# Order of the first loads and weights, and x added image by image, in a preactivation convolution on one core

## The chip, the cores and the metric

The kernel runs on one core of a Trainium2 chip. The metric is the device time of one execution in microseconds (us). Engines: TensorE (PE, matmuls; PEld, its weight loads), VectorE (DVE), ScalarE (ACT), GpSimd (POOL) and SyncE (SP, here only a queue that issues DMAs). ACT and POOL issue DMAs as well.

## The reference

x is 8 images of 32 channels, 64 x 64, float32. Each channel of each image is normalised over its pixels (a group norm with 32 groups of one channel), the image is split into its four parities (2 x 2 pixels become 4 x 32 = 128 channels of 32 x 32), and three depthwise convolutions (1x1, 3x3, 5x5) are joined to 384 features, projected by a 1x1 convolution to 128 channels, put back to 64 x 64, and added to x.

```python
g = (v - mean(v)) / sqrt(var(v) + 1e-5)                    # per image and channel
xd = concat([g[:, :, 0::2, 0::2], g[:, :, 0::2, 1::2], g[:, :, 1::2, 0::2], g[:, :, 1::2, 1::2]], axis=1)
feats = concat([dwconv(xd, w1, 1), dwconv(xd, w3, 3), dwconv(xd, w5, 5)], axis=1)
y = einsum('bchw,oc->bohw', feats, w_proj[:, :, 0, 0])
out[:, :, 0::2, 0::2], out[:, :, 0::2, 1::2], out[:, :, 1::2, 0::2], out[:, :, 1::2, 1::2] = split(y, 4, axis=1)
return x + out
```

## The kernel before

**Work.** The depthwise taps and the projection are folded where that pays. For the nine inner taps (distance at most 1) effective weights `weff` (projection scaled by w5, plus w3, for the centre also w1) are made on the chip and split into a high part `whi` and a low part `wlo`; the normalised image G is split into HI and LO in the same way, and PE accumulates HI x whi, HI x wlo and LO x whi: 3 x 9 taps x 2 banks of 512 columns = 54 matmuls an image (lines 657 to 706). The 16 outer taps of the 5x5 (the ring) are summed elementwise: ACT makes a scaled product for each of POOL's taps (line 430), POOL adds them into RING_SUM (line 316), DVE adds its own taps into ACC (lines 584, 592, 596), then F = ACC + RING_SUM (line 602), and PE projects F with one matmul a bank (`ring`, line 708). `POOL_N` says how many of the 16 taps of each image are POOL's, the first of them made by ACT straight into RING_SUM.

**Data.** X holds all images on the chip, two images to a pair t = b // 2 (64 partitions each, even rows on the first 32 of them, odd rows on the others). ACT copies the finished YP of image b into Y (`copy_y`, line 406; Y has room for two pairs), POOL starts a DMA that adds Y to X for a pair (`add_x`, line 322, places in `ADD_X_AT`: after sum (4, 2), (6, 2) and (7, 6)), and SP stores both images of the pair when it has landed (lines 246 to 249). Image 6 is added by POOL itself in two halves (lines 344 to 349), image 7 by DVE from PSUM (lines 620 to 626); each half is stored when it is done, by SP and, for half of image 7, by ACT. SP's stores are issued in the order of the program: pairs 0, 1, 2, then image 6, then image 7.

**Start.** Image 0's and image 1's statistics come from a second copy of the images, the parts XS (four parts of each channel on 128 partitions), by `part_bn`, a mask (`spread`) and a PE matmul (`sum_parts`, line 643); POOL takes the root by pow (`inv_std`), and DVE makes the bias (`part_bias`, line 500). SP issues w5, w3, the parts of image 0 in two pieces, the parts of image 1, images 1 to 7. ACT issues the projection, w1 and image 0. PE transposes the projection, then the coefficients (line 726), then sums the parts; `keep_warm` and the loop of line 732 are matmuls without a use in the result, as many as `WARM` says. ACT scales nine weight tiles by w5 (`scale_w5`, line 370), then waits for image 0 and its bias, makes three of the four pieces of HI of image 0 (`high_half`, line 379; DVE makes the other at line 560), then G (`normalise`). DVE adds w3 and w1 and casts whi in three chunks of three taps; POOL makes wlo. `high(0)` on PE takes bank and chunk alternately: (0,0), (1,0), (0,1), (1,1), (0,2), (1,2).

**Order.** Each engine runs its own program in order; semaphores link them. DVE interleaves statistics of later images with the taps of image 0 (the table `between`, line 610). POOL starts the DMA that makes LO of image b+1 after three sums of image b (`NEXT_IMAGE_AT`).

Of the kernel before, what the change touches and what calls it, by code (L numbers as in the profile page):

```python
# [5 lines left out]
ALU = mybir.AluOpType  # L6
# [28 lines left out]
POOL_N = [5, 6, 6, 6, 7, 7, 7, 8]  # L35
# [10 lines left out]
ADD_X_AT = [(4, 2), (6, 2), (7, 6)]  # L46
# [3 lines left out]
WARM = (7, 2, 2, 8)  # L50
CHUNK = 3
CHUNKS = N_INNER // CHUNK
PARTS = 4
# [5 lines left out]
AREAS = 3  # L59
RING_AFTER_HIGH = {2: 0, 3: 1, 4: 2, 5: 3, 6: 4, 7: 6}  # L60
# [33 lines left out]
def build(nc, x, w1, w3, w5, wp, out):  # L94
    with ExitStack() as ctx:  # L95
# [64 lines left out]
        wt_ready, wpT_ready = sem("wt_ready"), sem("wpT_ready")  # L160
        w5_scaled, weff_step = sem("w5_scaled"), sem("weff_step")
# [12 lines left out]
        row_added = [sem(f"row_added{t}") for t in range(PAIRS - 1)]  # L174
# [57 lines left out]
        def _(sp):  # L232
            sp.dma_start(w_sb[:, 0:W3_AT], w5.rearrange("c a h w -> c (a h w)")).then_inc(w_loaded, 16)
            sp.dma_start(w_sb[:, W3_AT:W1_AT], w3.rearrange("c a h w -> c (a h w)")).then_inc(w_loaded, 16)
            load_parts(sp, 0, 0, 512, xs_loaded[0])
            load_parts(sp, 0, 512, 1024, xs_loaded[1])
            load_parts(sp, 1, 0, 1024, xs_loaded[2])
# [8 lines left out]
            for t in range(PAIRS - 1):  # L246
                sp.wait_ge(row_added[t], 16)
                store(2 * t, 0, PH)
                store(2 * t + 1, 0, PH)
# [9 lines left out]
        def _(pool):  # L259
# [46 lines left out]
            def sum_products(b):  # L306

                pool.wait_ge(first_prod, b + 1)
                for k in range(N_PROD[b]):
                    if k == NEXT_IMAGE_AT and b + 1 < B:  # L310
                        low_image(b + 1)
                    pool.wait_ge(prod_ready, products_before(b) + k + 1)
                    if k > 0:
                        pool.wait_ge(prod_added, products_before(b) + k)
                    dst = part(RING_SUM[:, b % SUMS, :, :], POOL_OF[b][k + 1])
                    pool.tensor_tensor(dst, dst, prod(b, k), ALU.add).then_inc(prod_added, 1)  # L316
                    if (b, k) in ADD_X_AT:
                        add_x(ADD_X_AT.index((b, k)))
                    if (b, k) in INV_STD_AT:
                        inv_std(*INV_STD_AT[b, k])  # L320

            def add_x(t):

                pool.wait_ge(y_copied, 4 * (t + 1))
                pool.dma_start(X[:, t, :, :].rearrange("p h w -> p (h w)"),
                               Y[:, t % 2, :, :, :].rearrange("p h w j -> p (h w j)"),
                               accum_op=ALU.add).then_inc(row_added[t], 16)

            inv_std(1, 0, 1)
            pool.wait_ge(whi_ready, CHUNKS)  # L330
# [21 lines left out]
        def _(act):  # L352
            act.dma_start(wp_sb[:, :], wp.rearrange("o c a b -> o (c a b)")).then_inc(wp_loaded, 16)
            act.dma_start(w_sb[:, W1_AT:N_COEF], w1.rearrange("c a h w -> c (a h w)")).then_inc(w_loaded, 16)
            load_image(act, 0, image_loaded[0])
# [19 lines left out]
            scale_w5(0, 6)  # L375
            copy_wpT(0)
            scale_w5(6, N_INNER)
# [28 lines left out]
            def copy_y(b):  # L406

                act.wait_ge(conv_done, b + 1)
                if b >= 4:
                    act.wait_ge(row_added[b // 2 - 2], 16)  # L410
# [34 lines left out]
            high_half(0, TOP, 0, hi_top)  # L445
            high_half(TOP, PH, 0, hi_bottom)
# [14 lines left out]
        def _(dve):  # L461
# [67 lines left out]
            def add_w3(*taps):  # L529

                for n in taps:
                    dve.wait_ge(w5_scaled, n + 1)
# [96 lines left out]
        def _(pe):  # L629
# [38 lines left out]
            def high(b):  # L668

                if b == 0:  # L670
                    pe.wait_ge(hi_top, 2)
                    for bank, k in ((0, 0), (1, 0), (0, 1), (1, 1), (0, 2), (1, 2)):
# [50 lines left out]
            for _ in range(WARM[1]):  # L723
                keep_warm(ident[:, :], P)
            pe.wait_ge(w_loaded, 48)
            nc.tensor.matmul(COEF_PS, ident_ph[:, :], w_sb[:, :], start=True, stop=True).then_inc(coef_ready, 1)
            for _ in range(WARM[2]):
                keep_warm(ident[:, :], P)
            sum_parts(0)
# [30 lines left out]
```

## Time and profile before

| | us |
|---|---|
| time, median of 3 runs | 147.44 (147.08 to 148.12) |
| the profiled execution, its own time | 148.02 |
| its span, first to last instruction | 146.2 |
| PE / DVE / ACT / POOL busy | 129.3 / 125.1 / 109.1 / 111.5 |
| mean granted clock of PE | 0.955 of full |

The busy times say how full an engine is, not what the end waits for; for that one reads the timeline at both ends, with the idle time in front of a group in square brackets and what ended it. Times within the profile count from the start of the span. Durations below come from the one profiled execution.

### The profile page before, as it was taken

The numbers are of one execution on the slowest core, as the hardware profiler recorded it, in microseconds if no ns is written. First come the engines' busy times: TensorE is split into PE (matmuls) and PEld (weight loads), VectorE is DVE, ScalarE is ACT, GpSimd is POOL, SyncE is SP. The second block draws the span as 40 slices with busy tenths as digits, with TensorE's granted clock in tenths as the row PEclk, the third lists the DMA queues.
The fourth block names the chain that finished last, engine by engine and source line by source line (L and its number), as shares of the span: only waits on it lengthen the run. The fifth ranks groups of instructions, "written<-read, shape, count | busy, mean of one in ns | idle before, by whom it ended". The sixth has DMA issues, their size and how long they took to land.

```text
span 146.2 us, 1541 instructions
## 1 busy us (share of the span) xinstructions
PE 129.3 (88%) x507; PEld 97.5 (67%) x507; DVE 125.1 (86%) x153; ACT 109.1 (75%) x113; POOL 111.5 (76%) x81
## 2 busy tenths in 40 slices
PE   5963999999999999999999999999999996996500
PEld 5941878887877677767776777677766773783200
DVE  7467838989999999999999999999999999997700
ACT  1377973999999999999999999899989970500000
POOL 6110686979999999997989998999999999992000
PEclk9998579999999999999999999999999999999965
DMA  3999999707034034025019995700399920094997
GB/s 72 255 241 197 198 206 209 118 15 141 2 76 78 0 74 83 0 57 95 0 31 184 205 194 116 152 0 0 72 215 173 209 57 0 4 215 97 200 192 157
DMA packets 35799, 16.78 MB, mean 115 GB/s; under 512 B 34000, under 2 KB 34128, under 8 KB 35408
## 3 DMA queue, kind: packets, MB, share of 16 engines
q1 hardware_dynamic: 30928, 8.67, 31.0%
q0 software_dynamic: 1440, 7.04, 24.8%
q10 hardware_dynamic: 3424, 0.98, 3.3%
q8 instruction: 4, 0.07, 0.2%
q14 instruction: 3, 0.02, 0.1%
HBM read 5.46 MB, written 4.19 MB: 66 GB/s over the span
## 4 chain that ended last, share of the span: by engine, by line
PE 55%; DVE 17%; POOL 8%; DMA 7%; ACT 3%; issue 3%; ACTq 1%; DVEq 0%; POOLq 0%
PE YP L665 49%; DVE ACC L592 11%; POOL RING_SUM L316 7%; DMA X<-in_x_dram 7%; PE YP L716 6%; DVE F L602 3%; DVE ACC L584 2%; DVE ACC L596 2%; ACT HI L382 2%; ACT Y L413 1%; ACT PROD L430 1%; POOL LO L303 1%; DVEq L95 0%; DVE X L626 0%; ACTq L217 0%
## 5 line engine op out<-in xcount | busy, mean ns | idle before, releaser
L316 POOL TENSOR_TENSOR RING_SUM<-RING_SUM,PROD 128x900 f32<-128x900 f32 (+1 forms) x44 | 89.1, 2037 | 5.1 <-ACT PROD L430 0.8
L592 DVE SCALAR_TENSOR_TENSOR ACC<-G,coef,ACC 128x930 f32<-128x930 f32 (+1 forms) x60 | 71.6, 1194 | 1.9
L430 ACT ACTIVATE PROD<-G,coef 128x900 f32<-128x900 f32 (+1 forms) x44 | 43.7, 1057 | 0.0
L665 PE MATMUL YP<-HI,whi 128*128 128x512 f32 (+1 forms) x144 | 38.8, 425 | 3.1 <-ACT HI L382 3.1
L665 PE MATMUL YP<-HI,wlo 128*128 128x512 f32 (+1 forms) x144 | 38.3, 419 | 0.0
L665 PE MATMUL YP<-LO,whi 128*128 128x512 f32 (+1 forms) x144 | 36.9, 407 | 0.0
L665 PEld LDWEIGHTS YP<-HI,whi 128*128 128x128 f32 x144 | 29.1, 204 | 11.5 <-ACT HI L382 3.0
L665 PEld LDWEIGHTS YP<-HI,wlo 128*128 128x128 f32 x144 | 27.3, 190 | 9.2 <-issue 2.9
L665 PEld LDWEIGHTS YP<-LO,whi 128*128 128x128 f32 x144 | 27.2, 190 | 7.7 <-issue 1.0
L392 ACT ACTIVATE G<-X,nbias,rstd 64x1024 f32<-64x1024 f32 x16 | 21.1, 1318 | 3.8 <-DVE nbias L503 3.2
L413 ACT ACTIVATE Y<-YP 64x1024 f32<-64x1024 f32 x14 | 15.3, 1091 | 7.0 <-PE YP L716 6.7
L716 PE MATMUL YP<-F,wpT 128*128 128x512 f32 x32 | 15.4, 598 | 2.6 <-DVE F L602 2.6
L716 PEld LDWEIGHTS YP<-F,wpT 128*128 128x128 f32 x32 | 5.9, 189 | 7.6 <-DVE F L602 3.5
L584 DVE TENSOR_SCALAR ACC<-G,coef 128x1024 f32<-128x1024 f32 x8 | 10.3, 1288 | 0.5 <-ACT G L392 0.3
L602 DVE TENSOR_TENSOR F<-ACC,RING_SUM 128x1024 f32<-128x1024 f32 x8 | 9.8, 1224 | 0.3
L596 DVE SCALAR_TENSOR_TENSOR ACC<-G,coef,ACC 128x930 f32<-128x930 f32 (+1 forms) x8 | 9.6, 1206 | 0.2
L423 ACT ACTIVATE RING_SUM<-G,coef 128x1024 f32<-128x1024 f32 x8 | 9.1, 1144 | 0.1
L285 POOL TENSOR_TENSOR rstd<-vare,mhalf 128x1 f32<-128x1 f32 (+1 forms) x4 | 2.4, 604 | 7.0 <-DVE vare L498 6.3
L403 ACT ACTIVATE LO<-HI 128x1024 fp32r<-128x1024 f32 x7 | 7.5, 1073 | 0.2
L401 ACT ACTIVATE HI<-G 128x1024 fp32r<-128x1024 f32 x7 | 7.5, 1069 | 0.2
L333 POOL TENSOR_TENSOR wlo<-weff,whi 128x384 fp32r<-128x384 f32 x3 | 3.0, 1010 | 6.0 <-DVE whi L540 6.0
L485 DVE BATCH_NORM_STATS2 st<-X 128x6 f32<-128x512 f32 x12 | 7.4, 680 | 0.0
(61 smaller groups left out, 64.3 us busy)
## 6 DMA issues: line engine op xcount, KB each, us to landing
LO<-G POOLq DMA_DIRECT2D x7, 543.0 KB, 4.9
X<-in_x_dram SPq DMA_DIRECT2D x14, 256.0 KB, 5.4
X<-Y POOLq DMA_DIRECT2D x3, 1024.0 KB, 7.0
out_dram<-X SPq DMA_DIRECT2D x12, 256.0 KB, 4.7
out_dram<-X SPq DMA_DIRECT2D x6, 128.0 KB, 3.1
XS<-in_x_dram SPq DMA_DIRECT2D x2, 256.0 KB, 4.3
X<-in_x_dram ACTq DMA_DIRECT2D x2, 256.0 KB, 8.2
XS<-in_x_dram SPq DMA_DIRECT2D x1, 512.0 KB, 8.1
```

Of the source, the lines that this page charges most:

```text
L316: pool.tensor_tensor(dst, dst, prod(b, k), ALU.add).then_inc(prod_added, 1)
L392: act.activation(g_image(b, r0, r1)[HALF * j:HALF * (j + 1)], rows[:, :, :, j], ACT.Identity, bias=nbias[p0:p0 + HALF, col(b):col(b) + 1], ...
L401: act.activation(s_image(HI, b), g_image(b), ACT.Copy).then_inc(hi_ready, 1)
L413: act.activation(Y[p0:p0 + HALF, b // 2 % 2, :, :, j], YP[HALF * j:HALF * (j + 1), b % AREAS, :].rearrange("p (h w) -> p h w", w=PW), ACT. ...
L423: act.activation(RING_SUM[:, b % SUMS, :, :], g_tap(b, POOL_OF[b][0], True), ACT.Copy, scale=of5(POOL_OF[b][0])).then_inc(first_prod, 1)
L430: act.activation(prod(b, k), g_tap(b, POOL_OF[b][k + 1]), ACT.Copy, scale=of5(POOL_OF[b][k + 1])).then_inc(prod_ready, 1)
L584: dve.tensor_scalar(ACC[:, :, :], g_tap(b, tap, True), of5(tap), None, ALU.mult).then_inc(acc_step, 1)
L592: dve.scalar_tensor_tensor(part(ACC, tap), g_tap(b, tap), of5(tap), part(ACC, tap), ALU.mult, ALU.add).then_inc(acc_step, 1)
L596: dve.scalar_tensor_tensor(part(ACC, tap), g_tap(b, tap), of5(tap), part(ACC, tap), ALU.mult, ALU.add).then_inc(late_done, 1)
L602: dve.tensor_tensor(f_image, ACC[:, :, :], RING_SUM[:, b % SUMS, :, :], ALU.add).then_inc(f_ready, 1)
L665: mm = nc.tensor.matmul(dst, w[:, n, :], src, start=start, stop=False, skip_group_check=True)
L716: mm = nc.tensor.matmul(YP[:, b % AREAS, cols], wpT[:, 2, :], F[:, b % 2, cols], start=False, stop=True, skip_group_check=True)
```

## The change

SP issues the two pieces of image 0's parts first, then image 0, then the parts of image 1 and images 1 to 7; w5 and w3 move to ACT's queue behind the projection, image 0 leaves it. On PE the part sums of image 0 come before the coefficients' transpose, with the two warming matmuls between, nine zero matmuls follow instead of eight, and `high(0)` takes (0,1) before (1,0). ACT scales three tiles at first, three more and copies the last part of the transposed projection after the first piece of HI; POOL scales the last three tiles. In image 0 one tap goes from DVE to POOL. `add_x` works on one image (64 partitions) at (3,0), (4,0), (5,0), (6,0), (7,0) and (7,4), each with a semaphore of its own, and SP stores image by image.

```diff
@@ -32,7 +32,7 @@
 INNER = [(0, -1), (0, 1)] + [(dy, dx) for dy in (-1, 1) for dx in (-1, 0, 1)] + [(0, 0)]
 RING = [(dy, dx) for dy in range(-2, 3) for dx in range(-2, 3) if max(abs(dy), abs(dx)) == 2]
 POOL_TAPS = [(0, 2), (-2, -2), (-2, 2), (2, -2), (2, 2), (-2, -1), (2, 1), (-1, -2)]
-POOL_N = [5, 6, 6, 6, 7, 7, 7, 8]
+POOL_N = [6, 6, 6, 6, 7, 7, 7, 8]
 POOL_OF = [POOL_TAPS[:n] for n in POOL_N]
 DVE_FIRST = (0, -2)
 DVE_OF = [[DVE_FIRST] + [t for t in RING if t not in POOL_OF[b] + [DVE_FIRST]]
@@ -43,13 +43,13 @@
 PROD_SIZE = max((PH - abs(dy)) * (PW - abs(dx)) for taps in POOL_OF for dy, dx in taps[1:])
 LATE = tuple(range(8))
 
-ADD_X_AT = [(4, 2), (6, 2), (7, 6)]
 N_PADS = 7
 PRODS = 10
 TOP = BANK_ROWS + 1
-WARM = (7, 2, 2, 8)
+WARM = (7, 2, 2, 9)
 CHUNK = 3
 CHUNKS = N_INNER // CHUNK
+ACT_SCALED = 6
 PARTS = 4
 STATS = 12
 COLS = 2 + PAIRS - 1
@@ -57,6 +57,8 @@
 SLOTS = 4
 HELD = 3
 AREAS = 3
+ADD_X_AT = {(b + AREAS, 0): b for b in range(B - AREAS)}
+ADD_X_AT[(7, 4)] = 5
 RING_AFTER_HIGH = {2: 0, 3: 1, 4: 2, 5: 3, 6: 4, 7: 6}
 COMBINE_AT = {(0, 8): (1, 1, 2), (1, 0): (2, 2, PAIRS)}
 RING_AFTER_WLO = {6: 5}
@@ -158,6 +160,7 @@
         const_step, pads_zero = sem("const_step"), sem("pads_zero")
         permuted, hi_top, hi_bottom = sem("permuted"), sem("hi_top"), sem("hi_bottom")
         wt_ready, wpT_ready = sem("wt_ready"), sem("wpT_ready")
+        pool_scaled = sem("pool_scaled")
         w5_scaled, weff_step = sem("w5_scaled"), sem("weff_step")
         whi_ready, wlo_ready = sem("whi_ready"), sem("wlo_ready")
         bn_done, agg_done, comb_done = sem("bn_done"), sem("agg_done"), sem("comb_done")
@@ -171,7 +174,7 @@
         last_bank = sem("last_bank")
         inner_done, conv_done, y_copied = sem("inner_done"), sem("conv_done"), sem("y_copied")
         half_added, last_added, stored = sem("half_added"), sem("last_added"), sem("stored")
-        row_added = [sem(f"row_added{t}") for t in range(PAIRS - 1)]
+        row_added = [sem(f"row_added{b}") for b in range(B - 2)]
 
         def image(tile, b, at, rows):
 
@@ -230,10 +233,9 @@
 
         @block.sync
         def _(sp):
-            sp.dma_start(w_sb[:, 0:W3_AT], w5.rearrange("c a h w -> c (a h w)")).then_inc(w_loaded, 16)
-            sp.dma_start(w_sb[:, W3_AT:W1_AT], w3.rearrange("c a h w -> c (a h w)")).then_inc(w_loaded, 16)
             load_parts(sp, 0, 0, 512, xs_loaded[0])
             load_parts(sp, 0, 512, 1024, xs_loaded[1])
+            load_image(sp, 0, image_loaded[0])
             load_parts(sp, 1, 0, 1024, xs_loaded[2])
             load_image(sp, 1, image_loaded[1])
             for b in range(2, B):
@@ -243,10 +245,9 @@
                 for i in range(2):
                     store_rows(sp, b, i, r0, r1)
 
-            for t in range(PAIRS - 1):
-                sp.wait_ge(row_added[t], 16)
-                store(2 * t, 0, PH)
-                store(2 * t + 1, 0, PH)
+            for b in range(B - 2):
+                sp.wait_ge(row_added[b], 16)
+                store(b, 0, PH)
             for half in range(2):
                 sp.wait_ge(half_added, half + 1)
                 store(B - 2, half * BANK_ROWS, (half + 1) * BANK_ROWS)
@@ -315,18 +316,23 @@
                     dst = part(RING_SUM[:, b % SUMS, :, :], POOL_OF[b][k + 1])
                     pool.tensor_tensor(dst, dst, prod(b, k), ALU.add).then_inc(prod_added, 1)
                     if (b, k) in ADD_X_AT:
-                        add_x(ADD_X_AT.index((b, k)))
+                        add_x(ADD_X_AT[b, k])
                     if (b, k) in INV_STD_AT:
                         inv_std(*INV_STD_AT[b, k])
 
-            def add_x(t):
-
-                pool.wait_ge(y_copied, 4 * (t + 1))
-                pool.dma_start(X[:, t, :, :].rearrange("p h w -> p (h w)"),
-                               Y[:, t % 2, :, :, :].rearrange("p h w j -> p (h w j)"),
-                               accum_op=ALU.add).then_inc(row_added[t], 16)
+            def add_x(b):
+
+                p0, t = HALF * (b % 2), b // 2
+                pool.wait_ge(y_copied, 2 * (b + 1))
+                pool.dma_start(X[p0:p0 + HALF, t, :, :].rearrange("p h w -> p (h w)"),
+                               Y[p0:p0 + HALF, t % 2, :, :, :].rearrange("p h w j -> p (h w j)"),
+                               accum_op=ALU.add).then_inc(row_added[b], 16)
 
             inv_std(1, 0, 1)
+            pool.wait_ge(wpT_ready, 1)
+            pool.wait_ge(coef_copied, 1)
+            for n in range(ACT_SCALED, N_INNER):
+                pool.tensor_scalar(weff[:, n, :], wpT[:, 2, :], of5(INNER[n]), None, ALU.mult).then_inc(pool_scaled, 1)
             pool.wait_ge(whi_ready, CHUNKS)
             for k in range(CHUNKS):
                 taps = slice(k * CHUNK, (k + 1) * CHUNK)
@@ -351,8 +357,9 @@
         @block.scalar
         def _(act):
             act.dma_start(wp_sb[:, :], wp.rearrange("o c a b -> o (c a b)")).then_inc(wp_loaded, 16)
+            act.dma_start(w_sb[:, 0:W3_AT], w5.rearrange("c a h w -> c (a h w)")).then_inc(w_loaded, 16)
+            act.dma_start(w_sb[:, W3_AT:W1_AT], w3.rearrange("c a h w -> c (a h w)")).then_inc(w_loaded, 16)
             act.dma_start(w_sb[:, W1_AT:N_COEF], w1.rearrange("c a h w -> c (a h w)")).then_inc(w_loaded, 16)
-            load_image(act, 0, image_loaded[0])
 
             def copy_wpT(k):
                 act.activation(wpT[:, k, :].rearrange("p (j i o) -> p j i o", j=2, i=2),
@@ -372,9 +379,7 @@
                     act.activation(weff[:, n, :], wpT[:, 2, :], ACT.Copy,
                                    scale=of5(INNER[n])).then_inc(w5_scaled, 1)
 
-            scale_w5(0, 6)
-            copy_wpT(0)
-            scale_w5(6, N_INNER)
+            scale_w5(0, CHUNK)
 
             def high_half(r0, r1, j, done):
 
@@ -407,7 +412,7 @@
 
                 act.wait_ge(conv_done, b + 1)
                 if b >= 4:
-                    act.wait_ge(row_added[b // 2 - 2], 16)
+                    act.wait_ge(row_added[b - 4], 16)
                 p0 = HALF * (b % 2)
                 for j in range(2):
                     act.activation(Y[p0:p0 + HALF, b // 2 % 2, :, :, j],
@@ -443,6 +448,8 @@
             act.wait_ge(image_loaded[0], 32)
             act.wait_ge(stats_ready, 1)
             high_half(0, TOP, 0, hi_top)
+            scale_w5(CHUNK, ACT_SCALED)
+            copy_wpT(0)
             high_half(TOP, PH, 0, hi_bottom)
             high_half(TOP, PH, 1, hi_ready)
             normalise(0, 0, PH, g_ready)
@@ -529,7 +536,10 @@
             def add_w3(*taps):
 
                 for n in taps:
-                    dve.wait_ge(w5_scaled, n + 1)
+                    if n < ACT_SCALED:
+                        dve.wait_ge(w5_scaled, n + 1)
+                    else:
+                        dve.wait_ge(pool_scaled, n - ACT_SCALED + 1)
                     dve.scalar_tensor_tensor(weff[:, n, :], wpT[:, 1, :], coef[:, w3_col(INNER[n]):w3_col(INNER[n]) + 1],
                                              weff[:, n, :], ALU.mult, ALU.add).then_inc(weff_step, 1)
 
@@ -669,7 +679,7 @@
 
                 if b == 0:
                     pe.wait_ge(hi_top, 2)
-                    for bank, k in ((0, 0), (1, 0), (0, 1), (1, 1), (0, 2), (1, 2)):
+                    for bank, k in ((0, 0), (0, 1), (1, 0), (1, 1), (0, 2), (1, 2)):
                         pe.wait_ge(whi_ready, k + 1)
                         if bank == 1 and k == 0:
                             pe.wait_ge(hi_bottom, 1)
@@ -722,11 +732,11 @@
 
             for _ in range(WARM[1]):
                 keep_warm(ident[:, :], P)
+            sum_parts(0)
+            for _ in range(WARM[2]):
+                keep_warm(ident[:, :], P)
             pe.wait_ge(w_loaded, 48)
             nc.tensor.matmul(COEF_PS, ident_ph[:, :], w_sb[:, :], start=True, stop=True).then_inc(coef_ready, 1)
-            for _ in range(WARM[2]):
-                keep_warm(ident[:, :], P)
-            sum_parts(0)
             pe.wait_ge(low_zero, 1)
             zeros = LO[:, SLOTS - 1, :]
             for _ in range(WARM[3]):
```

## Rows read from the trace of the kernel before

**Rows 1.** The page, busy us of each engine (share of the span) and instructions.

```profile
PE 129.3 (88%) x507; PEld 97.5 (67%) x507; DVE 125.1 (86%) x153; ACT 109.1 (75%) x113; POOL 111.5 (76%) x81
```

**Rows 2.** Timeline of PE, late: start, us, engine, line, operation, [idle before, releaser].

```profile
123.36 1.98 PE L716 MATMUL YP<-F,wpT 128*128 128x512 f32 x4 [1.22 <-DVE F L602]
...
134.59 1.13 PE L716 MATMUL YP<-F,wpT 128*128 128x512 f32 x2 [1.35 <-DVE F L602]
```

**Rows 3.** Timeline of VectorE, its last additions.

```profile
137.32 1.41 DVE L626 TENSOR_TENSOR X<-YP,X 64x512 f32<-64x512 f32 x2 [0.15 <-PE YP L716]
```

**Rows 4.** Timeline of SyncE's queue at the end.

```profile
133.53 10.56 SPq L229 DMA_DIRECT2D out_dram<-X  x10
...
143.48 0.61 SPq L229 DMA_DIRECT2D out_dram<-X  x1
```

**Rows 5.** The page's DMA issues: count, KB each, median us to landing.

```profile
LO<-G POOLq DMA_DIRECT2D x7, 543.0 KB, 4.9
...
X<-Y POOLq DMA_DIRECT2D x3, 1024.0 KB, 7.0
...
X<-in_x_dram ACTq DMA_DIRECT2D x2, 256.0 KB, 8.2
```

**Rows 6.** Timeline of GpSimd, an issue in mid-stream and the end.

```profile
52.23 0.88 POOL L303 DMA_DIRECT2D LO<-G  x1
52.85 10.56 POOL L316 TENSOR_TENSOR RING_SUM<-RING_SUM,PROD 128x900 f32<-128x900 f32 x5
...
105.22 21.43 POOL L316 TENSOR_TENSOR RING_SUM<-RING_SUM,PROD 128x900 f32<-128x900 f32 x10
...
127.67 4.75 POOL L349 TENSOR_TENSOR X<-X,Y 64x1024 f32<-64x1024 f32 x2 [0.22 <-ACT Y L413]
```

**Rows 7.** Windows: us, busy PE, PEld, DVE, ACT, POOL (x), PEclk, DMA share, GB/s.

```profile
135.00:136.00 1.00, 1.00 (x4) 0.57 (x3) 0.25 (x1) 0.00 (x0) 0.00 (x0) 1.00 0.91 201
```

**Rows 8.** Timeline of VectorE at the start.

```profile
5.55 0.69 DVE L491 BATCH_NORM_STATS2 stp<-XS 128x6 f32<-128x512 f32 x1 [1.18 <-DMA XS<-in_x_dram]
...
7.70 0.21 DVE L548 TENSOR_TENSOR spread<-stp,mask 128x48 f32<-128x48 f32 x1
...
9.78 0.22 DVE L503 TENSOR_SCALAR nbias<-agg,rstd 128x1 f32<-128x1 f32 x1
...
22.51 0.38 DVE L496 BATCH_NORM_AGGREGATE agg<-YP 128x2 f32<-128x48 f32 x1 [2.82 <-PE YP L647]
...
29.83 0.16 DVE L513 COPY mean<-YP 128x1 f32<-128x1 f32 x1 [0.69 <-PE YP L653]
```

**Rows 9.** Timeline of ScalarE at the start.

```profile
7.12 1.86 ACT L372 ACTIVATE weff<-wpT,coef 128x128 f32<-128x128 f32 x6
...
11.97 2.44 ACT L382 ACTIVATE HI<-X,nbias,rstd 64x544 fp32r<-64x544 f32 x3 [1.94 <-DMA X<-in_x_dram]
...
14.44 2.71 ACT L392 ACTIVATE G<-X,nbias,rstd 64x1024 f32<-64x1024 f32 x2
```

**Rows 10.** Windows, two microseconds within the first matmuls of image 0.

```profile
16.00:18.00 2.00, 2.00 (x6) 1.63 (x5) 1.70 (x3) 1.97 (x2) 1.81 (x3) 0.50 1.24 192
```

**Rows 11.** Timeline of PE, first matmuls of image 0 and first of image 1.

```profile
12.90 1.12 PE L665 MATMUL YP<-HI,whi 128*128 128x512 f32 x3 [2.60 <-ACT HI L382]
...
14.56 6.32 PE L665 MATMUL YP<-HI,whi 128*128 128x512 f32 x15 [0.54 <-ACT HI L382]
...
29.65 4.54 PE L665 MATMUL YP<-HI,whi 128*128 128x512 f32 x18
```

**Rows 12.** Timeline of SyncE's queue at the start.

```profile
0.74 0.40 SPq L233 DMA_DIRECT2D w_sb<-in_L_conv_w_dram  x1
...
1.66 1.42 SPq L222 DMA_DIRECT2D XS<-in_x_dram  x3
```

**Rows 13.** Timeline of GpSimd, low halves of two chunks of weights.

```profile
17.18 1.98 POOL L333 TENSOR_TENSOR wlo<-weff,whi 128x384 fp32r<-128x384 f32 x2
```

**Rows 14.** The page's costliest groups: busy, mean ns | idle before.

```profile
L592 DVE SCALAR_TENSOR_TENSOR ACC<-G,coef,ACC 128x930 f32<-128x930 f32 (+1 forms) x60 | 71.6, 1194 | 1.9
```

## The prediction

> **What bounds the kernel now.** I read the page's busy line, then the end by PE, DVE and SyncE's queue, then the start by timeline. PE is busy for 88% of the span and VectorE (DVE) for 86%, no engine for all of it [rows 1]. The end is set in two steps. First DVE: it delivers the last ring image F at 134.5, and PE can start the last ring matmul only then [rows 2]; DVE's last add ends at 138.73 [rows 3]. Then the DMAs: SyncE (SP) issues its last ten stores from 133.5 on [rows 4], because the accumulate of images 4 and 5 (1 MB, 7.0 us to landing [rows 5]) is issued by GpSimd (POOL) only after its last product, which ends at 126.65 [rows 6]. 2 MB of output are then left, at 201 GB/s [rows 7] some 10.4 us. The last store is issued at 143.48 and the span ends 2.7 us after it, at 146.2. So 7.5 us lie behind the last arithmetic.
>
> At the start all engines wait: DVE for image 0's parts until 5.55 and for PE's sums of image 1's parts until 22.51 (2.82 us) [rows 8]; ScalarE (ACT) for image 0's x until 11.97 [rows 9]; PE 2.60 us for the same at 12.90. Then PE's clock is granted at half (0.50, the 1.2 GHz level [rows 10]) and 15 matmuls take 6.32 us, where later 18 take 4.54 [rows 11]. From 29.83 to 134.5 DVE hardly pauses, so what its start gains reaches the end if nothing else binds.
>
> **The parts' load.** Two weight issues ahead of it leave SP's queue, so the parts are issued 0.9 us earlier (0.74 for 1.66) [rows 12] and the first statistic moves from 5.55 to 4.65. The second gains 0.9 for the same reason, or up to 1.6 since image 0's x no longer runs beside it; I take 1.4: the spread comes at 6.3 for 7.70. Image 0's x leaves ACT's queue, where it took 8.2 us to land [rows 5], for SP's, behind 512 KB of parts. 1 MB from about 2 us on, at 200 GB/s, has landed near 7.5. The loads of images 1 to 7 keep their order and the bytes ahead of them; images 2 and 3 are complete after 3.2 MB, by 18, and DVE will want them at 21.5.
>
> The Trainium skill (DMA: Bandwidth & Descriptors, Issuing engines are not separate DMA queues) says that DMAs of all issuing engines run on the same 16 engines and interleave, whoever starts them. By that rule the move to SP brings order and no bandwidth, and the sum stays as it is; what the trace shows, 8.2 us for 256 KB beside SP's loads, agrees.
>
> **Coefficients and first weights.** PE now sums the parts before it transposes the coefficients, with two warming matmuls between. The variance is ready near 7.45 and, with the 0.8 that lie before the bias today (pow on POOL), rstd at 8.2. The part sums take PE from 6.5 to 6.9, two warming matmuls 0.4, the coefficients 0.5 and ACT's copy of them 0.3: ACT starts scaling at 8.05 for 7.12, 0.9 later; at 0.31 each (1.86 for six [rows 9]) the third is ready at 9.0. DVE's first three adds stand ahead of the bias in its queue; the last ends 0.3 after that. So the bias comes at 9.3 for 9.78, and image 0 is normalised from 9.6 for 11.97: 2.4 gained. It is then the bias that ACT waits for; x has 2 us to spare.
>
> The other three ACT scalings and a transposed copy (four of 0.3, 1.2 us) lay inside ACT's wait for x and now lie behind the first piece of HI. ACT: first piece to 10.4, scalings and copy to 11.65, two more pieces at 0.8 to 13.3, G to 16.05 for 17.15 [rows 9]. Gain 2.4 less 1.2. DVE: its piece of HI to 10.65, adds 3 to 5 paced by ACT to 11.75, cast, four adds of 0.3 and a cast: whi is complete at 13.65, some 2 us early, since the HI pieces and casts are. POOL's three scalings are not in the trace. From below nothing (it idles there), from above 0.99 us each, as its subtraction on a tile three times as wide [rows 13]. I take 0.33, nearest by size; but even 3.0 us from 8.2 end at 11.2, before DVE asks at 12. Cost 0.
>
> **PE.** It starts on bank 0 at 10.7, takes bank 0's second chunk at 12.15 (the new order, else it would stand for bank 1 until 13.3), and bank 1 at 13.3. With one warming matmul more and the earlier start its longest idle shrinks from 2.60 to about 0.7 us. I take the clock as staying full. At 0.25 each [rows 11] the last 12 matmuls end at 16.3 for 20.88 and the six of wlo at 17.85; image 1's parts are summed by 18.2. DVE comes for them at 18.55 (16.05, plus 1.3 and 1.2): its 2.82 us of waiting go and it is 3.95 early. At 29.83 it had waited for PE again [rows 8]; PE is 4.0 early there too, so 4.0 are carried on.
>
> The Trainium skill (TensorE: Matmul & The Clock Gate, What's actually happening) says that the clock is gated down by default, that activity releases it, and that the moment of the change varies from run to run. The trace shows it fall after idle and return under work. By that rule the broken-up work from 10 to 13.3 might still end in half clock; what that costs is rival 1.
>
> **One ring tap from DVE to POOL in image 0.** DVE saves 1.2 [rows 14], ACT pays 1.0 in a later gap of its own, POOL 2.1 (five in 10.56 [rows 6]). DVE's total gain is 4.0 + 1.2 = 5.2. PE's is 4.0; it waited 1.22 us for F of image 6 at 123.36 [rows 2], and with F 5.2 earlier that wait goes, so PE too is ready for the last F.
>
> **x added image by image.** Six issues on POOL for three. 1 MB lands in 7.0 us, 543 KB in 4.9 [rows 5]; 512 KB take some 4.7. What an issue costs POOL: from below 0.62 (issue at 52.23, next sum at 52.85), from above 1.0 (126.65 to 127.67) [rows 6]. I take 0.62, the row of an issue between two sums: six are 3.7 for two of 1.0 ahead of the last sum today, +1.7. POOL starts its sums 3.5 earlier (its own start work is not 3.95 ahead), so its last product ends at 126.65 - 3.5 + 2.1 + 1.7 = 126.9, or 124.5 if the 2.4 us in which it stood for ACT, PE or an issue pair go. DVE asks at 128.1: cover 1.2 to 3.6. Each issue at 1.0 would take 2.3 of it. Behind the wait for y_copied stand POOL's next sum and LO issue, and for LO PE; but Y is copied on ACT ahead of the same image's products, and for image 5 right behind ACT's last product, some 4 us before POOL gets there. It holds nothing.
>
> Stores of images 0 to 5 go out from about 62 us on, the last by 128. POOL's adds for image 6 (4.75 [rows 6]) end between 129.4 and 131.7, and their 512 KB are gone by 134.5.
>
> **The sum.** F at 129.3; last add 138.73 - 5.2 = 133.5; from its store to the end of the span 2.7, and 0.6 (0 to 1.3) because the last 512 KB come close together: span 136.8. The profiled execution took 148.02, 1.8 above its span: 138.6. The median of the runs, 147.44, is 0.4% under the profiled one, by which it would be 138.1; I keep 138.6.
>
> **Rivals.**
> 1. The clock still falls at 13.6. Then 12 matmuls and the six of wlo at 0.42 end at 20.8; DVE goes on at 21.1, and PE is only 1.1 early when DVE waits for it at 29.83. DVE gains 1.1 + 1.2 for 5.2, and the end is 2.9 later: 141.5. For it: PE pauses three times from 10 to 13.3. Against: no pause is long.
> 2. The start brings nothing (weights late behind the reordered PE, moved scalings in ACT's way), so that part of the change doesn't do what it says. Tap and stores remain: 138.73 - 1.2 + 2.7 + 0.6 + 1.8 = 142.6. Against: ACT is 1.1 ahead even with the scalings.
> 3. POOL becomes the bound, with issues at 1.0: 126.9 + 2.3 = 129.2 and F 1.1 to 1.3 late: 139.9.
> 4. The other side: an accumulate holds POOL until it has landed, 4.7 each. Six cost 28 us for 3.7, less a cover of some 4: F comes 20 later, 159. It decides from 0.6 us more per issue on; slower than before from about 2.2 more. Against: today's issues of 1 MB cost 1.0, not 7.0.
>
> **How the numbers follow.** Forecast 0.55, rival 1 0.22, rival 2 0.09, rival 3 0.08, rival 4 0.03, and 0.03 for no measurable change through mishaps not named. About 1% is what a measurement of this kernel can tell from no change. The first four are all faster by over 3%: faster 0.94, same 0.03, slower 0.03. Low end: 138.1 by the median, less the 0.6 of the last stores and 0.2 for the second part at its best, 137.3. High end: rival 1 and 0.7 for the last stores at their worst, 142.2; that leaves out rivals 2 and 4.
>
> **What would show it.** Right: image 0's spread near 6.3; ACT's HI from 9.6, released by the bias; clock 1.00 from 13 to 20; no PE wait at DVE's second aggregate (18.6); F of image 7 ending at 129.3; the last store issued within 1 us of DVE's last add; POOL's sums 0.6 apart around an issue. Wrong: clock 0.50 after 13.6; POOL as releaser of F; stores still working off a backlog at 135; PE waiting for LO.

## The result and the profile after

The changed kernel takes 139.71 us (median of 4 runs, 139.31 to 140.82) beside 147.26 us for the kernel before: ratio 0.9504 with a 95% interval of 0.9418 to 0.9589, 7.5 us less. The forecast was 138.6 (137.3 to 142.2). The profiled execution took 139.66 us with a span of 137.8, where the forecast had 136.8. In this ratio and in all that follow, executions more than 1.5% above the fastest of the same kernel are left out.

The busy line and the DMA issues of the page answer to [rows 1, 5]:

```profile
PE 126.6 (92%) x508; PEld 94.8 (69%) x508; DVE 123.9 (90%) x152; ACT 109.1 (79%) x111; POOL 117.6 (85%) x88
...
LO<-G POOLq DMA_DIRECT2D x7, 543.0 KB, 5.3
X<-Y POOLq DMA_DIRECT2D x6, 512.0 KB, 7.2
```

The span is 8.4 us shorter; POOL does 6.1 us more work in it, the others nearly the same. The last line is unlike the forecast: 512 KB take 7.2 us to land, not 4.7.

VectorE by timeline, start and end, answers to [rows 3, 8]:

```profile
4.83 0.50 DVE L471 COPY wp_ph<-wp_sb 128x128 f32<-128x128 f32 x3 [0.89 <-DMA wp_sb<-in_L_conv_w_proj_dram]
...
6.55 0.21 DVE L558 TENSOR_TENSOR spread<-stp,mask 128x48 f32<-128x48 f32 x1
...
9.58 0.20 DVE L510 TENSOR_SCALAR nbias<-agg,rstd 128x1 f32<-128x1 f32 x1
...
16.11 1.29 DVE L594 TENSOR_SCALAR ACC<-G,coef 128x1024 f32<-128x1024 f32 x1 [0.91 <-ACT G L397]
...
18.56 0.37 DVE L503 BATCH_NORM_AGGREGATE agg<-YP 128x2 f32<-128x48 f32 x1
...
25.62 0.16 DVE L520 COPY mean<-YP 128x1 f32<-128x1 f32 x1 [0.16 <-PE YP L663]
...
127.87 1.23 DVE L612 TENSOR_TENSOR F<-ACC,RING_SUM 128x1024 f32<-128x1024 f32 x1
...
131.89 1.41 DVE L636 TENSOR_TENSOR X<-YP,X 64x512 f32<-64x512 f32 x2 [0.15 <-PE YP L726]
```

The part sums' wait of 2.82 us is gone at 18.56 (no bracket), the spread comes at 6.55, the bias at 9.58, and the last F starts at 127.87 and ends at 129.10. The last addition ends at 133.30, 5.4 us earlier than before.

ScalarE and PE at the start, PE late, and a windows row answer to [rows 2, 9, 10, 11]:

```profile
8.23 0.99 ACT L379 ACTIVATE weff<-wpT,coef 128x128 f32<-128x128 f32 x3
9.90 0.88 ACT L387 ACTIVATE HI<-X,nbias,rstd 64x544 fp32r<-64x544 f32 x1 [0.68 <-DVE nbias L510]
...
13.40 2.67 ACT L397 ACTIVATE G<-X,nbias,rstd 64x1024 f32<-64x1024 f32 x2
```

```profile
7.73 2.31 PE L743 MATMUL YP<-LO 128*128 128x512 f32 x9
10.97 0.98 PE L675 MATMUL YP<-HI,whi 128*128 128x512 f32 x3 [0.93 <-DVE HI L570]
...
12.49 4.16 PE L675 MATMUL YP<-HI,whi 128*128 128x480 f32 x15 [0.53 <-DVE whi L550]
...
117.92 1.98 PE L726 MATMUL YP<-F,wpT 128*128 128x512 f32 x4
...
129.15 1.13 PE L726 MATMUL YP<-F,wpT 128*128 128x512 f32 x2 [1.35 <-DVE F L612]
```

```profile
10.00:20.00 10.00, 8.48 (x35) 6.23 (x35) 8.70 (x18) 9.89 (x13) 6.52 (x8) 1.00 1.37 197
```

ACT scales from 8.23, starts HI at 9.90 (11.97 before), released by the bias and no more by a DMA, and ends G at 16.07. PE's clock is 1.00 from 10 to 20. Fifteen matmuls take 4.16 us for 6.32, and ring(6) at 117.92 waits for nothing; the last ring waits 1.35 us for F as before.

GpSimd by timeline, and SyncE's queue at the start and the end, answer to [rows 4, 6, 12]; the windows row (columns as in [rows 7]) shows the last stores under way:

```profile
8.57 2.21 POOL L335 TENSOR_SCALAR weff<-wpT,coef 128x128 f32<-128x128 f32 x3
...
119.87 0.80 POOL L327 DMA_DIRECT2D X<-Y  x1
120.46 4.43 POOL L317 TENSOR_TENSOR RING_SUM<-RING_SUM,PROD 128x930 f32<-128x930 f32 x2
124.84 4.71 POOL L355 TENSOR_TENSOR X<-X,Y 64x1024 f32<-64x1024 f32 x2
```

```profile
0.73 0.87 SPq L225 DMA_DIRECT2D XS<-in_x_dram  x2
...
127.70 6.90 SPq L232 DMA_DIRECT2D out_dram<-X  x8
```

```profile
134.00:135.00 1.00, 0.00 (x0) 0.00 (x0) 0.00 (x0) 0.00 (x0) 0.00 (x0) 1.00 1.04 216
```

The parts' issue is at 0.73 for 1.66. POOL scales three tiles in 2.21 us and ends its last product at 124.89. Image 5's accumulate is issued at 119.87 and its stores start at 127.70. From then on the queue has 1.5 MB to write and works until between 136 and 137, so the span ends 4.5 us after DVE's last addition and not 3.3.

### The profile page after: what moved, and what is told of

It reads as the page before. It is cut to its first block, busy times and chain, and to the rows that moved or that the text cites. A ratio compares the mean times of both kernels' runs of the same rounds, so it can differ in the third digit from the quotient of the medians.

```text
span 137.8 us, 1549 instructions
## 1 busy us (share of the span) xinstructions
PE 126.6 (92%) x508; PEld 94.8 (69%) x508; DVE 123.9 (90%) x152; ACT 109.1 (79%) x111; POOL 117.6 (85%) x88
## 4 chain that ended last, share of the span: by engine, by line
DVE 76%; PE 12%; DMA 3%; issue 3%; ACT 1%; DVEq 1%; ACTq 0%
DVE ACC L602 48%; PE YP L675 10%; DVE ACC L606 7%; DVE ACC L594 7%; DVE F L612 6%; DVE st L492 3%; DMA wp_sb<-in_L_conv_w_proj_dram 3%; PE YP L726 1%; DVE weff L543 1%; DVE stp L498 1%; ACT HI L387 1%; DVEq L97 1%; ACT weff L379 1%; DVE X L636 0%; PE YP L657 0%
## 5 line engine op out<-in xcount | busy, mean ns | idle before, releaser
L317 POOL TENSOR_TENSOR RING_SUM<-RING_SUM,PROD 128x900 f32<-128x900 f32 (+1 forms) x45 | 92.6, 2065 | 3.4
L602 DVE SCALAR_TENSOR_TENSOR ACC<-G,coef,ACC 128x930 f32<-128x930 f32 (+1 forms) x59 | 70.4, 1194 | 1.8
L435 ACT ACTIVATE PROD<-G,coef 128x900 f32<-128x900 f32 (+1 forms) x45 | 44.7, 1057 | 0.0
L675 PE MATMUL YP<-HI,whi 128*128 128x512 f32 (+1 forms) x144 | 36.4, 404 | 1.5 <-DVE HI L570 0.9
L675 PEld LDWEIGHTS YP<-HI,whi 128*128 128x128 f32 x144 | 27.0, 190 | 9.5 <-DVE HI L570 1.4
L606 DVE SCALAR_TENSOR_TENSOR ACC<-G,coef,ACC 128x930 f32<-128x930 f32 (+1 forms) x8 | 9.7, 1207 | 0.3
L304 POOL DMA_DIRECT2D LO<-G x7 | 6.4, 913 | 0.0
L643 PE MATMUL YP<-ident 128*128 128x128 f32 x22 | 4.6, 378 | 1.7 <-POOL ident L265 1.7
```

What stands on the lines that cost most here:

```text
L435: act.activation(prod(b, k), g_tap(b, POOL_OF[b][k + 1]), ACT.Copy, scale=of5(POOL_OF[b][k + 1])).then_inc(prod_ready, 1)
L602: dve.scalar_tensor_tensor(part(ACC, tap), g_tap(b, tap), of5(tap), part(ACC, tap), ALU.mult, ALU.add).then_inc(acc_step, 1)
L606: dve.scalar_tensor_tensor(part(ACC, tap), g_tap(b, tap), of5(tap), part(ACC, tap), ALU.mult, ALU.add).then_inc(late_done, 1)
L675: mm = nc.tensor.matmul(dst, w[:, n, :], src, start=start, stop=False, skip_group_check=True)
```

## The experiments

Ratios are to the kernel before on the same chip, with their 95% intervals. The runs fall in three groups, each on a chip of its own: the first four, the next four, the last four.

**1. Start and tap alone, x added by pairs.**

```diff
-ADD_X_AT = {(b + AREAS, 0): b for b in range(B - AREAS)}
-ADD_X_AT[(7, 4)] = 5
+ADD_X_AT = [(4, 2), (6, 2), (7, 6)]
...
-            for b in range(B - 2):
-                sp.wait_ge(row_added[b], 16)
-                store(b, 0, PH)
+            for t in range(PAIRS - 1):
+                sp.wait_ge(row_added[t], 16)
+                store(2 * t, 0, PH)
+                store(2 * t + 1, 0, PH)
```

> The changed kernel with x added and stored by pairs as before; start and tap as changed. Theory (start, tap and stores all needed): DVE ends its last add at 133.3 as in the changed kernel, but POOL issues the last 1 MB accumulate only after its last product, near 123.4, it lands 7 us later, and 2 MB of stores at 200 GB/s follow: span near 142.5, time near 144.3, half-way between the two kernels. Rival (the start is all that counts, the stores were hidden): within 1 us of the changed kernel, 139.7.

145.15 us, ratio 0.9865 (0.9826 to 0.9905). GpSimd, and VectorE's last additions:

```profile
123.02 0.88 POOL L326 DMA_DIRECT2D X<-Y  x1
```

```profile
130.29 2.97 DVE L635 TENSOR_TENSOR X<-YP,X 64x512 f32<-64x512 f32 x4 [1.22 <-PE YP L725]
```

DVE ends at 133.26 as in the changed kernel, but the span is 143.1: 9.8 us of stores stand behind. Of the 5.5 us that DVE gains, the span gains 3.1 and the ratio 2.0; without the other stores the rest is not paid out.

**2. The stores alone.** The kernel before with `add_x`, its places, its semaphores and SP's stores by image, as in the change.

```diff
-ADD_X_AT = [(4, 2), (6, 2), (7, 6)]
+ADD_X_AT = {(b + AREAS, 0): b for b in range(B - AREAS)}
+ADD_X_AT[(7, 4)] = 5
```

> The kernel before with only x added and stored image by image. Theory: DVE's last add stays at 138.7 and the stores end some 4 us behind it: span near 143, time near 144.8, about 3 us faster than before. Rival (six issues make POOL late): F of image 7 waits for POOL, time 146 or more.

142.95 us, ratio 0.9721 (0.9650 to 0.9792), more than either theory gave:

```profile
21.79 0.38 DVE L497 BATCH_NORM_AGGREGATE agg<-YP 128x2 f32<-128x48 f32 x1 [1.26 <-PE YP L648]
...
135.03 2.97 DVE L627 TENSOR_TENSOR X<-YP,X 64x512 f32<-64x512 f32 x4 [1.22 <-PE YP L717]
```

DVE's last addition ends at 138.00, 0.7 us earlier than in the profile before, with no part of the start changed (DVE waited 1.26 us there for 2.82, PE having its full clock back sooner), and the span (141.2) ends 3.2 us after it: no backlog. POOL's six issues make nothing late. By the ratios the stores alone give 4.1 us, the start and the tap alone 2.0, and both together (0.9504) 7.3; by the profiled spans 5.0, 3.1 and 8.4. So the two parts add up, nearly: what the ratios have above the sum, 1.2 us, is no more than the intervals allow, and the spans show 0.3. Each part leaves a limit standing that the other removes, but that together they give more than their sum is not shown.

**3. The tap back on DVE.**

```diff
-POOL_N = [6, 6, 6, 6, 7, 7, 7, 8]
+POOL_N = [5, 6, 6, 6, 7, 7, 7, 8]
```

> The changed kernel with image 0's tap back on DVE (POOL_N 5). Theory A (DVE sets the end): DVE's last add 1.2 later, time near 140.9. Theory B (the end is the work-off of the last 1.5 MB of stores, which POOL's last accumulate starts): POOL is 2.1 earlier, the stores start earlier, and the time stays within 0.4 of 139.7.

140.55 us (140.47 to 140.70), ratio 0.9561 (0.9513 to 0.9609), between the two theories. VectorE's bias and last additions, PE's zero matmuls, and POOL's issue for image 5:

```profile
10.74 0.20 DVE L510 TENSOR_SCALAR nbias<-agg,rstd 128x1 f32<-128x1 f32 x1
```

```profile
132.70 2.97 DVE L636 TENSOR_TENSOR X<-YP,X 64x512 f32<-64x512 f32 x4 [1.22 <-PE YP L726]
```

```profile
8.75 3.35 PE L743 MATMUL YP<-LO 128*128 128x512 f32 x9
```

```profile
119.86 0.83 POOL L327 DMA_DIRECT2D X<-Y  x1
```

DVE ends at 135.67, 2.4 us later: 1.2 for the tap, and 1.2 because the bias came at 10.74 and not 9.58. PE was slow there: its nine zero matmuls took 3.35 us for 2.31 (7.73 in the trace of the changed kernel). Yet the span is only 1.1 longer, for it ends 3.2 us after DVE. The other 1.3 is the backlog of stores: POOL, late by the start but with a product less to add, issues image 5's accumulate at 119.86, as in the changed kernel (119.87), and the later DVE hides what is left of it. A late start alone hides nothing: in experiments 4 and 11 DVE ends 1.2 and 1.7 us later than in the changed kernel, and the span 1.1 and 1.7. So the 1.1 us here may be all of the start. An estimate from these rows: with the bias at 9.58 DVE would end at 134.5 and the span at 137.7, where the changed kernel has 137.8. The tap saves 1.2 us on DVE, and what it gives at the end, while image 5's accumulate stays where it is, lies between nothing and 1.1.

**4. Fewer warming matmuls.**

```diff
-WARM = (7, 2, 2, 9)
+WARM = (7, 2, 2, 1)
```

> The changed kernel with one zero matmul instead of nine ahead of image 0 (they compute nothing). PE then idles some 3 us before its first piece of HI. Theory: the granted clock falls to half soon after 13 us as before the change, image 0's matmuls end some 2.5 us later, DVE waits 2 to 2.5 us for image 1's part sums, time near 142.3. Rival (the clock has no part in it): time unchanged, 139.7, clock 1.00 throughout or DVE not waiting.

140.89 us, ratio 0.9601 (0.9535 to 0.9667). PE, VectorE at its second aggregate and at the end, and the clock (the third number from the right, as in [rows 10]):

```profile
11.02 6.87 PE L675 MATMUL YP<-HI,whi 128*128 128x512 f32 x18 [2.76 <-DVE HI L570]
```

```profile
19.54 0.38 DVE L503 BATCH_NORM_AGGREGATE agg<-YP 128x2 f32<-128x48 f32 x1 [0.77 <-PE YP L657]
...
133.12 1.41 DVE L636 TENSOR_TENSOR X<-YP,X 64x512 f32<-64x512 f32 x2
```

```profile
10.00:16.00 6.00, 4.98 (x11) 3.59 (x12) 4.92 (x13) 5.92 (x9) 2.51 (x5) 0.50 1.36 206
```

The clock fell as expected, but PE got it back from 16 on, before the last of image 0's first pass; DVE waited 0.77 and 0.72 us for PE, and the end came 1.1 later in the profile, not 2.6. DVE ends at 134.53 and the span, 138.9, 4.4 behind it: the backlog is still there. Here some seven microseconds of half clock, part of them in PE's gaps, cost no more than the three of experiment 6: the time at which the clock is given back decides.

**5. The changed kernel again**, beside experiments 6 to 8.

> The changed kernel once more, beside the next three on one chip. Expected 139.7 within 0.6, the same landing of 7.2 us for the 512 KB accumulates, and stores that work off a backlog from 127.7 until the end.

140.68 us (139.56 to 141.05), ratio 0.9515 (0.9462 to 0.9569). The median is outside what was expected, the ratio is that of the first comparison (0.9504), and the executions fall into two groups. All ten of the changed kernel, with the mean granted clock of each:

```
clock 0.990 to 0.993:  139.31 139.56 139.60 139.66 139.76
clock 0.977 to 0.985:  140.33 140.82 141.03 141.04 141.05
```

Half of them took about 1.3 us longer, with more time at half clock. The mean counts the end too, where PE has nothing left to do: in the changed kernel's trace the clock is 1.00 until 135 and 0.50 from 136 on, and that alone makes its 0.990. No execution of the lower group was profiled; the trace of experiment 6 stands for it.

**6. Image 5's accumulate two sums earlier.**

```diff
-ADD_X_AT[(7, 4)] = 5
+ADD_X_AT[(7, 2)] = 5
```

> Image 5's accumulate two sums earlier, after (7,2) instead of (7,4). Theory (the end is the work-off of stores that begins when image 5's accumulate lands): it is issued near 115.7, lands near 123.4, its stores are gone before image 6's; the last add stays at 133.3 and the end comes 3.2 behind it instead of 4.5: 1.0 to 1.3 us faster than the changed kernel. Rival (the last stores are slow for themselves): no change within 0.3.

139.58 us (138.31 to 139.72) for 140.68, ratio 0.9437 (0.9388 to 0.9486). The profiled execution had the lower clock (0.981). PE, VectorE, and the clock:

```profile
12.38 5.53 PE L675 MATMUL YP<-HI,whi 128*128 128x480 f32 x15 [0.53 <-DVE whi L550]
```

```profile
19.57 0.38 DVE L503 BATCH_NORM_AGGREGATE agg<-YP 128x2 f32<-128x48 f32 x1 [0.97 <-PE YP L657]
```

```profile
131.60 2.97 DVE L636 TENSOR_TENSOR X<-YP,X 64x512 f32<-64x512 f32 x4 [1.22 <-PE YP L726]
```

```profile
14.00:16.00 2.00, 2.00 (x6) 1.61 (x5) 1.09 (x2) 1.97 (x2) 1.82 (x3) 0.50 1.34 211
```

The start is that of the changed kernel until 12.38; then fifteen matmuls take 5.53 us for 4.16, DVE waits 0.97 us for PE and ends at 134.57, 1.3 later. The span, 137.8, ends 3.2 us behind it, not 4.5. The best execution, 138.31, is 1.25 below the best of the changed kernel beside it, the median 1.1. The theory holds: the backlog of stores was worth what the forecast had missed.

**7. The same bytes on 128 partitions.** Two accumulates a pair, each over half the rows; the stores by pairs.

```diff
-                p0, t = HALF * (b % 2), b // 2
-                pool.wait_ge(y_copied, 2 * (b + 1))
-                pool.dma_start(X[p0:p0 + HALF, t, :, :].rearrange("p h w -> p (h w)"),
...
+                pool.wait_ge(y_copied, 4 * (t + 1))
+                rows = slice(half * BANK_ROWS, (half + 1) * BANK_ROWS)
+                pool.dma_start(X[:, t, rows, :].rearrange("p h w -> p (h w)"),
```

> The changed kernel with x added by pairs, each pair in two accumulates of 512 KB that cover half the rows of all 128 partitions, after (4,2) and (4,4), (6,2) and (6,4), (7,2) and (7,4). Theory (64 partitions take as long as 128, the duration goes by bytes per partition): each lands in 4.6 to 5.0 us like the 543 KB ones, against 7.2. Rival (half the size costs the same for another reason, such as the stores beside it): 7 us again. The time: 2 MB of stores from about 125.8 on at 200 GB/s end near 137, so 139 to 140 either way.

141.19 us, ratio 0.9548 (0.9489 to 0.9608). The page's DMA issues:

```profile
LO<-G POOLq DMA_DIRECT2D x7, 543.0 KB, 6.1
X<-Y POOLq DMA_DIRECT2D x6, 512.0 KB, 4.6
```

512 KB on 128 partitions land in 4.6 us, on 64 in 7.2. The stores beside it are not the reason: in the changed kernel the accumulate of image 0, issued at 57.2 with the first store only at 64.45, took 7.3 too. Per partition, 1 MB on 128 and 512 KB on 64 are the same bytes and take the same time (7.0 and 7.2), half of them 4.6. The time says little: the stores of images 4 and 5 wait for the pair here, and the start of the profiled execution was late as in experiment 3, for 1.1 us of its span of 139.5:

```profile
10.57 0.20 DVE L510 TENSOR_SCALAR nbias<-agg,rstd 128x1 f32<-128x1 f32 x1
```

**8. One more tap to POOL**, in image 1, with image 5 earlier as in 6.

```diff
-POOL_N = [6, 6, 6, 6, 7, 7, 7, 8]
+POOL_N = [6, 7, 6, 6, 7, 7, 7, 8]
```

> Image 5's accumulate after (7,2), and one tap of image 1 moved from DVE to POOL. Theory (DVE and the stores set the end, POOL has 3 us to spare for F of image 7): DVE's last F 1.2 earlier less at most 0.5 of waiting for POOL's last product, POOL's adds of image 6 end near 131.7, time 0.3 to 0.8 below the kernel with image 5 earlier alone. Rival (POOL's adds of image 6 become what the stores wait for): no gain over it, or a loss up to 0.5.

139.26 us (138.77 to 140.26), ratio 0.9437 (0.9384 to 0.9490), the same as experiment 6. The last F and POOL's additions for image 6, and the bias:

```profile
128.23 1.23 DVE L612 TENSOR_TENSOR F<-ACC,RING_SUM 128x1024 f32<-128x1024 f32 x1 [0.63 <-POOL RING_SUM L317]
```

```profile
128.06 4.67 POOL L355 TENSOR_TENSOR X<-X,Y 64x1024 f32<-64x1024 f32 x2
```

```profile
10.59 0.20 DVE L510 TENSOR_SCALAR nbias<-agg,rstd 128x1 f32<-128x1 f32 x1
```

Now POOL releases F (0.63 us) and its own additions end at 132.7. POOL's room is used up: this tap gains nothing that can be measured. The bias is a microsecond late once more, and this execution took 139.80 us with a mean clock of 0.997, where four others, at 0.988 to 0.991, took 138.77 to 139.35: a late start like this one does not show in the mean clock.

**9. Image 5 earlier and more warming.**

```diff
-WARM = (7, 2, 2, 9)
+WARM = (7, 4, 2, 12)
```

> Image 5's accumulate after (7,2), two more warming matmuls ahead of the part sums (in PE's wait of 0.57 us there) and twelve zero matmuls for nine (in its wait until 10.97). Theory (the 1.1 us by which executions of the changed kernel differ are a late rise or a short fall of PE's clock in the first 17 us): DVE's bias at 9.5 and no wait before its second aggregate in most executions, times close together at 138.3 to 138.6, median 1 below the kernel with image 5 earlier alone. Rival (the spread has another cause, or the clock doesn't answer to that little work): spread and median as there, 139.5.

138.73 us (138.15 to 140.12), ratio 0.9503 (0.9442 to 0.9563), the kernel before on that chip at 146.60. PE, and the bias on VectorE:

```profile
5.90 1.87 PE L643 MATMUL YP<-ident 128*128 128x128 f32 x8
7.60 0.32 PE L657 MATMUL YP<-spread,same 128*128 128x48 f32 x2
```

```profile
10.26 0.21 DVE L510 TENSOR_SCALAR nbias<-agg,rstd 128x1 f32<-128x1 f32 x1
```

The clock was full afterwards, but the added matmuls came ahead of the part sums while PE was slow (eight records in 1.87 us), and the sums went to 7.60 for 6.82, the bias to 10.26. The spread did not close: the mean clocks are all high, 0.990 to 1.000, and the times still lie 2 us apart, two executions with 1.000 taking 139.04 and 140.12 and two with 0.993 and 0.996 138.30 and 138.15. So half clock that the records show is not the whole cause of the spread. A late rise of the clock in the first microseconds, where the records read 1.00 anyhow, fits (experiments 3, 7 and 8); for the slow executions here no trace shows it. Whether it is better or worse than experiment 6 is not settled: on another chip its time is 0.85 lower and its ratio 0.0066 higher.

**10. The kernel before with more warming.**

```diff
-WARM = (7, 2, 2, 8)
+WARM = (7, 2, 2, 17)
```

> The kernel before with 17 zero matmuls instead of 8, which fill PE's wait for image 0's x. Theory (the half clock cost the kernel before part of the 5.3 us that the start won): clock 1.00 through image 0, DVE's wait of 2.82 us before 22.51 shrinks to about 0.7, all later work and POOL's last accumulate come 2 earlier, time near 145.4. Rival (the clock cost nothing there, PE waits for weights and x anyway): 147.4 within 0.5.

145.96 us, ratio 0.9958 (0.9913 to 1.0003). VectorE where it had waited 2.82 us:

```profile
20.22 0.38 DVE L496 BATCH_NORM_AGGREGATE agg<-YP 128x2 f32<-128x48 f32 x1 [0.37 <-PE YP L647]
```

The profile does what the theory says: the wait is 0.37 us and the span 144.0, 2.2 less than in the profile before. The median moves by 0.6 only. The profiled execution of the kernel before had a mean clock of 0.955; of the 17 executions of it beside this run only one had less (0.953), the others 0.956 to 0.983. So the trace on which the forecast rests had more half clock than most. As the ratio's interval takes in 1, it isn't shown that the usual execution gains from the matmuls.

**11. The loads in their old order**, PE kept busy.

```diff
             load_parts(sp, 0, 0, 512, xs_loaded[0])
             load_parts(sp, 0, 512, 1024, xs_loaded[1])
-            load_image(sp, 0, image_loaded[0])
...
+            load_image(act, 0, image_loaded[0])
```

(w5 and w3 are back ahead of the parts on SP, and 17 zero matmuls stand for 9.)

> The changed kernel with the loads in their old order (w5 and w3 ahead of the parts on SP, image 0's x on ACT) and 17 zero matmuls so that the clock has no part in it. Theory (the order of loads is worth the 2 us by which HI starts earlier): x lands near 11.9, HI of image 0 starts there instead of 9.9, DVE's first tap 2 later, time near 141.7. Rival (the reordering on PE, ACT and POOL gives the gain): within 0.7 of the changed kernel.

141.78 us, ratio 0.9703 (0.9614 to 0.9793). ScalarE's first piece of HI:

```profile
11.60 0.87 ACT L387 ACTIVATE HI<-X,nbias,rstd 64x544 fp32r<-64x544 f32 x1 [1.60 <-DMA X<-in_x_dram]
```

ACT waits 1.60 us for image 0's x; HI is 1.7 later than in the changed kernel, and the span 139.5 for 137.8. In the profiles the order of the loads is worth those 1.7 us; by the ratios (0.9703 for 0.9515, on two chips) it would be 2.8 with wide intervals.

**12. All scalings on ACT.**

```diff
-ACT_SCALED = 6
+ACT_SCALED = 9
```

> The changed kernel with the last three weight tiles scaled by ACT again, behind the first piece of HI, not by POOL. Theory: ACT's later HI pieces and G come 0.95 later, DVE's first tap too, time 0.6 to 1.0 above the changed kernel. Rival (DVE's adds and casts set G's reader, ACT has room): no change within 0.3.

Ratio 0.9648 (0.9558 to 0.9738), from two of four executions, 140.75 and 141.19 us. The profile is of one of the other two, 143.25 us, with half clock from 14 to 20. ScalarE and PE up to there:

```profile
10.99 1.85 ACT L379 ACTIVATE weff<-wpT,coef 128x128 f32<-128x128 f32 x6
```

```profile
14.70 5.38 PE L675 MATMUL YP<-HI,whi 128*128 128x512 f32 x12 [0.94 <-ACT HI L387]
```

Six scalings (1.85 us for 0.97) stand in front of the next pieces of HI, and PE waits 0.94 us for them, where it had waited for nothing. By the ratios the loss is 1.3% of 147, some 1.9 us, more than the 0.6 to 1.0 expected, but the intervals overlap (0.9515 goes up to 0.9569) and the chip is another. Shown is that three scalings on ACT make its pieces of HI and PE wait; that the move to POOL gains time at the end is likely by this and not shown by the times.

## Why the prediction was right, and where it was off

**What bounded it.** Right: two things, DVE and the stores behind POOL's last accumulate. Experiments 1 and 2 give each alone a part, and the parts come near the whole.

**The parts' load.** The spread came at 6.55 for 6.3. Missed: the projection's load now shares the DMAs with the parts, and DVE waited 0.89 us for it at 4.83. The 0.25 us pass on to the bias.

**Coefficients and first weights.** Bias 9.58 (9.3), HI 9.90 (9.6), released by the bias, G read at 16.11 (16.05). POOL's scalings took 0.74 each (2.21 for three), not 0.33, and stayed within the bounds and under cover, as worked out. Experiment 12 shows the wait that the move avoids.

**PE.** Right in the profile: last F 129.10 (129.3), no wait at DVE's second aggregate, and ring(6) meets F to the tenth. But "I take the clock as staying full" holds in only half of the executions. Rival 1 is not another outcome: it alternates with the forecast, and it costs 1.3 us and not 2.9. Its size was wrong because it had the half clock last to 20; in the traces it was given back after 16 (experiments 4 and 6), and DVE waited 0.97 us and ended 1.3 later. That three of the first four executions are of the group with the high clock is luck for the forecast: in experiment 5 it was two of six, with a median of 140.68, 2.1 above the forecast, though still in the range. The clock before was a matter of the execution as well: experiment 10 shows 2.2 us in the profile and 0.6 in the median.

A third kind of execution the forecast did not have: PE slow in its first microseconds, the bias at 10.57 to 10.74 and then full clock (experiments 3, 7 and 8), which costs DVE 1.0 to 1.2 us.

The Trainium skill (TensorE: Matmul & The Clock Gate, What's actually happening) says that the moment of the change varies from run to run. The runs here agree: one and the same program shows 0.977 to 0.993 as mean clock, and 1.3 us of difference in time go with it.

**The tap.** Worth 1.2 on DVE as forecast; at the end, where the forecast counted it in full, 1.1 at most and by the estimate in experiment 3 nothing, as the stores' backlog took its place. The cover on POOL was 3.0 us (last product ends at 124.89; DVE asked at 127.87), inside the forecast 1.2 to 3.6. A second tap used it up and brought nothing (experiment 8).

**x image by image.** The issues cost 0.57 to 0.6 us each, as taken (0.62). The step that failed is the size of one term: "512 KB take some 4.7". They took 7.2, the last 7.8, because an image lies on 64 partitions: the same bytes on all 128 landed in 4.6 (experiment 7), and 1 MB on 128 in 7.0. With that the allowance for the last stores, 0.6 (0 to 1.3), was too small as well: the trace has 1.8. So image 5's stores began at 127.70, 3 us later than they could, and 1.5 MB at some 200 GB/s filled the time to the end. Of the 1.0 us between 136.8 and 137.8, 1.2 are this, less 0.2 that DVE was better; experiment 6 takes it back by an earlier issue.

The row was there to be read more carefully: 543 KB of LO on 128 partitions were taken as a model for 512 KB on 64. The Trainium skill (SBUF — State Buffer, Door 1: The DMA port swizzle) says that partitions 0 to 63, and likewise 64 to 127, reach only half of the ports through which DMAs write, and gives 196 GB/s for 0 to 63 beside 328 for all 128 at 1 MiB, 1.7 times as long. The runs agree: 7.2 for 4.6 is 1.6 times; which port a packet took no run here shows.

**The rivals.** Rivals 2, 3 and 4 did not come: DVE's end was 5.4 earlier, F of image 7 did not wait for POOL, and an issue held POOL for 0.6 us.

**Best version.** Image 5's accumulate after (7,2) (experiment 6): 0.9437 (0.9388 to 0.9486) for the changed kernel's 0.9515 (0.9462 to 0.9569) beside it. The intervals overlap a little; the medians say 1.1 us, the executions with high mean clock 1.0 (138.31 and 138.81 for 139.56 and 139.60), those with 0.981 beside 0.977 to 0.978 1.4, and the trace says 1.3 between DVE's end and the end of the span.

## What to carry to other kernels

When the arithmetic is over and stores still run, ask which transfer opened that queue: here the issue of the last accumulates was worth 4 us and a place in POOL's program two sums earlier another 1.1. An accumulate on 64 partitions took as long here as twice its bytes on 128: compare by bytes per partition, not by bytes. What an engine saves is worth nothing at the end while the stores behind it are what ends last. And before a wait on PE is priced from one trace, look at the mean clock of several executions, and at the durations of the first matmuls, which that mean does not show.

## What the runs showed of the hardware

- An accumulate between two tiles on the chip: 7.0 us for 1 MB on 128 partitions, 4.6 for 512 KB on 128, 7.2 for 512 KB on 64.
- GpSimd multiplied a 128 x 128 tile by one value per partition in 0.74 us, ScalarE in 0.31 to 0.33.
- Executions of one program differ in how long PE's clock is at half in the first 20 us; in the trace with half clock after 13 us (experiment 6) DVE's end is 1.3 us later, and the changed kernel's two groups of executions lie 1.3 us of 140 apart.
- The windows' clock reads 1.00 in the first microseconds of every trace, also where nine matmuls took 3.35 us for 2.31 (experiment 3). There the durations show what the clock's rows do not.
